# Perceiver block: attention as one run over 128 batches, the work of three groups placed between its matmuls, and the 257th context row added once per group

## What is computed

```python
x = x + xattn(layernorm(x), ctx)      # 8 heads of 64; keys and values are the 257 context rows
x = x + decay(layernorm(x))           # per row: w,k,v,r projections and a scan over the 32 rows
x = x + ffn(layernorm(x))             # 256 -> 64 -> 1024 (gelu) -> 64 -> 256, bias b2

# xattn
attn = softmax((x @ Wq) @ (ctx @ Wk).T * 64**-0.5); out = (attn @ (ctx @ Wv)) @ Wo + bo
# decay, with its own layernorm inside (ln_g, ln_b)
state = (1 - w)[..., None] * state + k[..., None] * v[..., None, :]; out_t = r . state
```

## Time and profile before

| | |
|---|---|
| median of 3 runs | 1327.41 us (1326.62 to 1332.69) |
| the profiled execution's own time | 1328.87 us |
| its span, first to last instruction | 1327.1 us |
| mean granted TensorE clock | 0.972 |
| PE busy, 7368 matmuls | 1194.7 us, 90% of the span |
| DVE, ACT, POOL busy | 636.4 us (48%), 621.4 us (47%), 245.3 us (18%) |
| DMA | 73.85 MB, mean 56 GB/s |
| busiest lines on PE | L476 140.1, L440 132.2, L443 90.2, L480 85.9, L463 82.8 us |
| tail lines on PE | L454 58.8, L478 58.1, L481 51.4 us |

### The profile page before, as it was taken

How to read it: one execution, slowest core, us unless ns; L and a number is a source line. 1 busy time by engine, 2 the same in 40 slices (tenths; PEclk the granted TensorE clock), 3 DMA queues, 4 the chain that set the end, 5 groups by cost and what they waited for, 6 DMA issues and landing times.

```text
span 1327.1 us, 23547 instructions
## 1 busy us (share of the span) xinstructions
PE 1194.7 (90%) x7368; PEld 845.4 (64%) x7368; DVE 636.4 (48%) x2083; ACT 621.4 (47%) x1502; POOL 245.3 (18%) x276
## 2 busy tenths in 40 slices
PE   3889999998999999999999999999999999989865
PEld 2556666676666667666666766666666666766644
DVE  2326455363644536355462645536363553636442
ACT  2444463645546454453645446364543636455321
POOL 0012021121211212121121212112120211212030
PEclk9999999999999999999999999999999999999976
DMA  6212113030210302112030211203021130302000
GB/s 211 71 51 64 58 45 85 8 102 17 71 56 25 98 13 82 37 58 70 22 100 14 76 43 47 81 15 101 12 72 56 44 84 8 94 26 65 28 8 8
DMA packets 49684, 73.85 MB, mean 56 GB/s; under 512 B 5696, under 2 KB 31424, under 8 KB 49664
## 3 DMA queue, kind: packets, MB, share of 16 engines
q1 hardware_dynamic: 42464, 65.06, 17.0%
q10 hardware_dynamic: 7200, 8.53, 1.9%
HBM read 68.98 MB, written 4.59 MB: 55 GB/s over the span
## 4 chain that ended last, share of the span: by engine, by line
PE 40%; issue 36%; POOL 8%; ACT 8%; DVE 6%; ACTq 1%; DMA 0%; POOLq 0%; SPq 0%; DVEq 0%
PE gb L513 7%; PE gb L503 4%; PE scores L440 4%; PE gb L416 4%; PE scores L443 3%; POOL khat L1051 3%; PE gb L425 3%; PE gb L578 2%; PE acc L476 2%; PE ptp L463 2%; PE acc L480 2%; POOL rstd L1024 2%; POOL rhat L1043 2%; PE gb L569 1%; PE scores L454 1%
## 5 line engine op out<-in xcount | busy, mean ns | idle before, releaser
L662 ACT ACTIVATE probs<-scores,nmax 128x257 f32<-128x257 f32 x256 | 119.4, 472 | 209.8 <-DVE nmax L847 209.6
L847 DVE TENSOR_REDUCE nmax<-scores 128x1 f32<-128x257 f32 x256 | 96.9, 420 | 241.9 <-PE scores L454 135.9
L678 ACT ACTIVATE pc<-acc 128x512 f32<-128x512 f32 x128 | 76.5, 598 | 175.1 <-PE acc L481 175.1
L1024 POOL TENSOR_TENSOR rstd<-ve,vecs 128x2 f32<-128x2 f32 x48 | 35.3, 736 | 607.8 <-DVE ve L831 607.8
L476 PE MATMUL acc<-pt,raw_n 128*128 128x256 f32 x512 | 140.1, 396 | 0.6 <-ACT pt L674 0.6
L440 PE MATMUL scores<-raw_t,qk 128*128 128x257 f32 x512 | 132.2, 381 | 1.4 <-ACT qk L698 1.4
L945 DVE COPY_PREDICATED s<-mask,gb 128x256 f32<-128x256 uint8 x256 | 112.6, 442 | 13.7 <-issue 8.3
L463 PE MATMUL ptp<-ident_r,probs 128*128 128x128 f32 x512 | 82.8, 287 | 24.5 <-DVE probs L854 24.5
L476 PEld LDWEIGHTS acc<-pt,raw_n 128*128 128x128 f32 x512 | 90.9, 190 | 20.2 <-issue 3.2
L440 PEld LDWEIGHTS scores<-raw_t,qk 128*128 128x128 f32 x512 | 88.5, 190 | 9.3 <-issue 1.7
L674 ACT ACTIVATE pt<-ptp 128x512 f32<-128x512 f32 x128 | 76.0, 594 | 37.3 <-PE ptp L463 35.9
(11 more groups left out here) (117 smaller groups left out, 2405.0 us busy)
## 6 DMA issues: line engine op xcount, KB each, us to landing
raw_t<-in_ctx_t SPq DMA_DIRECT2D x128, 258.0 KB, 2.8
raw_n<-in_ctx_n SPq DMA_DIRECT2D x128, 192.0 KB, 2.3
xin<-in_x SPq DMA_DIRECT2D x16, 256.0 KB, 2.9
out<-vt ACTq DMA_DIRECT2D x16, 256.0 KB, 3.4
tailc<-tail_scratch SPq DMA_DIRECT2D x64, 6.0 KB
wq<-in_wq SPq DMA_DIRECT2D x1, 512.0 KB, 3.6
wk_raw<-in_wk SPq DMA_DIRECT2D x1, 512.0 KB, 4.1
wo<-in_wo ACTq DMA_DIRECT2D x1, 512.0 KB, 5.4
```

The source lines that it names most:

```text
L662: go(probs[:, r, 0:L], scores[:, r, 0:L], ACT.Exp, bias=nmax[:, r:r + 1], accum_out=rsum[:, r:r + 1]).then_inc(s["exp_ready"], 1)
L678: go(pc[:, :, :, b * S:(b + 1) * S], acc[:].rearrange("p c (h s) -> p c h s", h=H), ACT.Copy).then_inc(s["pc_ready"], 1)
L847: v_.tensor_reduce(nmax[:, r:r + 1], scores[:, r, 0:L], AX.X, ALU.max, negate=True)\
```

## The change

- The phases and the loop go. PE, ACT, DVE and POOL run through one unrolled sequence of slots (i, b), i from -1 to 17; while batch n = 8i+b has its attention, the slot's fills come from group i+1 (queries), i-1 (`WV Y1 XT2 z k r v Sa`) and i-2 (`Sb O2 Y2`, ffn).
- The block `START` goes: all its steps stand in `FILL1` and `FILL2`. Eight batches of attention follow the eight before them directly. The steps of DVE and POOL have tables of their own.
- The 257th row: `turn_tail`, `ptt`, L478, L481, `tail_parts` and the `tailc` loads go. In their place the values of all 257th rows (`VT`) are computed once; POOL sorts each batch's last column into `ptm` (`tail_column`, 32 elements a row); once per group PE turns it (`TP`, two products of 32 columns), DVE spreads it (`psp`) and `WV` gets four more products (K = 64, 256 columns) with `vsp`, which 16 small DMAs on SP fill per group.
- `nmaxs` becomes one reduction of 2x257, `norm_probs` one TENSOR_TENSOR with a broadcast `rinv` in place of two scalings. `probs`, `qk`, `x12` are double, `raw_t` and `raw_n` threefold, and all other tiles have memory of their own.
- The second power chain on POOL goes (the norm of a normed row is folded into epsilon). The softmax scale moves from `wk` to ACT's drain of `q`.
- ACT issues 24 loads at the start (`wq`, 8 small, 15 weights); SP issues the stores; `xb` has its own load.

```diff
-START = ["WV0", "WV1", "XT", "XT3", "Pf", "q0", "q1", "H0", "H1", "Y1", "Qk0", "Qk1", "q2", "H2", "H3", "Qk2", "Qk3",
-         "q3", "Qk4", "Qk5", "XT2", "Qk6", "Qk7", "z"]
-FILL1 = [["k"], ["r"], ["v"], ["Sa0", "Sa1"], ["Sa2", "Sa3"], ["Sb0", "Sb1"], ["Sb2", "Sb3"], ["O2"]]
-FILL2 = [["Y3"], [], [], [], [], [], [], ["Y2"]]
+FILL1 = [["WV"], ["Y1"], ["q0", "q1", "XT2"], ["z", "k"], ["r", "q3"], ["Qk2", "Qk4", "Pf"], ["v", "H0"],
+         ["TP", "Qf", "Sa0"]]
+FILL2 = [["Sb0"], ["Sb2", "XT"], ["q2", "O2"], ["Y2"], ["Qk0", "XT3"], ["Qk6"], ["H2"], ["Sa2", "Y3"]]
...
-                    if b > 0:
-                        turn_tail(b - 1, "scores_ready")
...
-                    mm(acc[:, 0], tailc[:, b % 4, 0:P], ptt[:], start=False, stop=True)
...
-                    last = mm(acc[:, 1], tailc[:, b % 4, P:2 * P], ptt[:], start=False, stop=True)
...
+            def turn_tails(g):
+                out_ = tile("TP", g)
+                pe.wait_ge(s["ptm_ready"], (g + 1) * G)
+                for r in range(2):
+                    last = mm(out_[:, 0, 0:S], ptm[g % 2][:, r].rearrange("p a b h -> p (a b h)"), diag[:],
+                              start=r == 0, stop=r == 1)
+                done("TP", g, last)
...
+                    last = [mm(out_[p][:, i], vsp[64 * p:64 * p + 64, (4 * p + 2 * i) * DH:(4 * p + 2 * i + 2) * DH],
+                               psp[64 * p:64 * p + 64].rearrange("p b s -> p (b s)"), start=False, stop=True)
+                            for p in range(2)]
...
+            for i in range(FIRST, LAST + 1):
+                for b in range(G):
+                    n = i * G + b
+                    before, behind = fills(i, b)
+                    if 0 <= n < B:
+                        turn_probs(n)
+                    if 0 <= n + 1 < B:
+                        score(n + 1)
+                    for name, g in before:
+                        steps[name](g)
+                    if 0 <= n < B:
+                        pv(n)
+                    for name, g in behind:
+                        steps[name](g)
...
+                for h in range(H):
+                    cols = slice(h * DH, (h + 1) * DH)
+                    for half in range(2):
+                        sp.dma_start(vsp[half * 64 + h:half * 64 + 64:H, cols], scratch[g * G:(g + 1) * G, cols])\
+                            .then_inc(vsp_in, 16)
...
+            for i in range(0, LAST + 2):
+                for b in range(G):
+                    n = i * G + b
+                    if b == 1 and 0 <= i - 3 < NG:
+                        store(i - 3)
+                    if b == 2 and i < NG:
+                        load_xb(i)
+                    if b == 5 and i < NG:
+                        load_tail_values(i)
+                    if b == 7 and i + 2 < NG:
+                        load_x(i + 2)
+                    if n + RING < B:
+                        load_t(n + RING)
+                        load_n(n + RING)
...
+            def nmaxs(n):
+                dve.wait_ge(s["scores_ready"], 2 * n + 2)
+                v_.tensor_reduce(nmax[:], scores[:, :, 0:L], AX.X, ALU.max, negate=True)\
+                    .then_inc(s["nmax_ready"], 1)
...
+                v_.tensor_tensor(p_[:, :, 0:L], p_[:, :, 0:L],
+                                 rinv[:].rearrange("p (r o) -> p r o", o=1).to_broadcast([P, 2, L]),
+                                 ALU.mult).then_inc(s["probs_ready"], 1)
...
+            GAPS = [[["Sa2-2", "Sa3-2"], [], ["Y3-3"]],
+                    [["Sb0-2", "Sb1-2"], [], ["Y1-1"]],
+                    [["xn1-1", "Sb2-2", "Sb3-2"], [], []],
+                    [[], [], ["f1-1", "f2-1", "f3-1", "i1-1", "i2-1"]],
+                    [["Y2-2"], ["xn2-2"], ["i3-1", "pw-1", "bw-1", "k1-1", "b1-1"]],
+                    [["p1-1"], [], ["b2-1"]],
+                    [["p2-1"], [], ["ln0+2"]],
+                    [["xn0+2"], ["psp+0"], ["Sa0-1", "Sa1-1"]]]
...
+                p_.tensor_tensor(ptm[g % 2][:, :, :, b],
+                                 probs[n % 2][:, :, L - 1:L].rearrange("p r (o u) -> p r o u", o=1)
+                                 .to_broadcast([P, 2, 2, H]), head[:], ALU.mult).then_inc(s["ptm_ready"], 1)
...
+            STEPS = [[[], []], [[], ["ln1-1"]], [[], []], [[], []], [["ln2-2"], ["k0-1", "xb+0"]],
+                     [["r1-1", "k2-1"], ["r0-1"]], [["r2-1", "k3-1"], ["ln0+2"]], [["r3-1"], ["ob-2"]]]
```

More of the change, by code:

```diff
@@ L74 @@
[L74 to L115, removed]
@@ L142 @@
-class Chain:
[L145 to L151, removed]
+RING = 3
+BANKS = 4
+PREP, HERE, POST, FFN = 1, 0, -1, -2
+FILL1 = [["WV"], ["Y1"], ["q0", "q1", "XT2"], ["z", "k"], ["r", "q3"], ["Qk2", "Qk4", "Pf"], ["v", "H0"],
+         ["TP", "Qf", "Sa0"]]
@@ new lines @@
+FILL2 = [["Sb0"], ["Sb2", "XT"], ["q2", "O2"], ["Y2"], ["Qk0", "XT3"], ["Qk6"], ["H2"], ["Sa2", "Y3"]]
+TILES = {"WV": ["WV0", "WV1"]}
+for pair in ("Qk0 Qk1", "Qk2 Qk3", "Qk4 Qk5", "Qk6 Qk7", "H0 H1", "H2 H3", "Sa0 Sa1", "Sa2 Sa3", "Sb0 Sb1",
+             "Sb2 Sb3"):
+    TILES[pair.split()[0]] = pair.split()
+SHIFT = {"XT": PREP, "TP": HERE}
+SHIFT.update({f"q{p}": PREP for p in range(4)})
+SHIFT.update({f"Qk{h}": PREP for h in range(H)})
+SHIFT.update({n: POST for n in "WV Y1 XT2 z k r v Sa0 Sa2".split()})
@@ L213, in build @@
[L213 to L219, removed]
+        qk = [sb(f"qk{i}", [P, 2, G, 256]) for i in range(2)]
+        pc = sb("pc", [P, 2, H, T])
+        ptm = [sb(f"ptm{i}", [P, 2, 2, G, H]) for i in range(2)]
@@ new lines, in build @@
+        psp = sb("psp", [P, G, S])
+        vsp = sb("vsp", [P, INNER])
+        xin, xn0, xt1 = sb("xin", [P, 2, D]), sb("xn0", [P, 2, D]), sb("xt1", [P, 2, T])
+        qs = sb("qs", [P, 4, T])
+        stats, mv = sb("stats", [P, 3, 2, 6]), sb("mv", [P, 3, 2, 2])
+        ve, rstd, half = sb("ve", [P, 3, 2]), sb("rstd", [P, 3, 2]), sb("half", [P, 2])
+        o_ = sb("o", [P, 4, T])
+        xb = sb("xb", [P, 2, D])
+        x12 = [sb(f"x12_{i}", [P, 2, D]) for i in range(2)]
+        xn1, xt2 = sb("xn1", [P, 2, D]), sb("xt2", [P, 2, T])
@@ new lines, in qf_, with y3 @@
+            def qf_(g):
+                out_ = tile("Qf", g)
+                drained("H3", g)
+                for c in range(8):
+                    r0 = 64 * (c % 2)
+                    last = mm(out_[r0:r0 + 64, 0], u2[:, c], hid[:, c], start=c < 2, stop=c > 5)
+                done("Qf", g, last)
+            def y3(g):
+                out_ = tile("Y3", g)
+                drained("Qf", g)
+                for t in range(2):
+                    last = mm(out_[:, t], qf[:, t * P:(t + 1) * P], v2[:], start=True, stop=True)
+                done("Y3", g, last)
@@ new lines, in wait_tile, with drain, exps @@
+            def wait_tile(name, g):
+                bank, k = BANK[name, g]
+                act.wait_ge(bank_filled[bank], k)
+                return gb[bank]
+            def drain(name, g, last):
+                last.then_inc(bank_drained[BANK[name, g][0]], 1)
+            def exps(n):
+                act.wait_ge(s["nmax_ready"], n + 1)
+                if n > 1:
+                    act.wait_ge(s["ptm_ready"], n - 1)
+                for r in range(2):
+                    go(probs[n % 2][:, r, 0:L], scores[:, r, 0:L], ACT.Exp, bias=nmax[:, r:r + 1],
+                       accum_out=rsum[:, r:r + 1]).then_inc(s["exp_ready"], 1)
```

1296 lines of the change are left out of this document (574 added, 722 removed).

## The result

| | before | changed |
|---|---|---|
| median of the runs, us | 1327.01 | 1265.2 (1261.3 to 1271.74) |
| ratio (95%) | | 0.9531 (0.9481 to 0.958) |
| profiled execution, its span, us | 1328.87, 1327.1 | 1261.3, 1259.2 |
| mean granted clock of the span | 0.972 | 0.957 |

A forecast was written before the change was run, and what follows sets the result against it. PE's passes, then exposed chains once per turn, were taken as the bound. 30.4 + 49.3 + 59.7 + 892 (13 full groups of 68.6) + 60.2 + 73 = 1164.6 us span, so 1165 us; range 1140 to 1192.

The forecast's parts named there:

- slot 5: In b=5 of a full group the maxima start some 1 us late and PE stands about 1.2 us at Pf.
- slot 7: In b=6 and 7 Qf waits 0.55 us for ACT's last gelu; in b=7 late x loses 0.2 us.
- the rival from SP: Sixteen vsp transfers on SP make PE wait from 0.94 us each; at 1.7 each, 1333 us; chance 0.03.
- the port rival: POOL hinders each batch's new scaling, 1.0 us later in 13 or so slots without cover: 1178 us; chance 0.04.
- the clock: Full groups: no wait as long as the 1.69 us behind which the granted clock fell, so no clock loss.
- the waits stay: In-order engines and a four-tile ring leave 6 us of waits in a group instead of 2: 1221 us; chance 0.18.
- the clock falls again: If PE's stand at b=5 nears 1.7 us, 1.7 us more per group: 1189 us; chance 0.05.
- The joints: PE's matmuls of a full group, switches priced as today: 66.6 us, 65 to 68 with more alternation.
- i = 1: Second group of attention, without ffn and Sb O2 Y2: 56.7 + 3 = 59.7 us.
- i = 15: Last group of attention, no queries to make, 8.4 us less: 60.2 us.
- i = 0: First group of attention, few fills, five slots as long as the softmax chain, late x costs 3: 49.3 us.
- The run-out: Behind the last attention, from WV on: 73 us (70 to 79), where today takes 76.4.

The follow-up runs named there:

- x2: Changed kernel with x of the group after next asked for at b = 0 instead of b = 7: 1232.43 us, 0.9264.
- x4: Changed kernel with three edits together (p1 behind the maxima of b = 5, x asked for at b = 0, Pf behind the product with the context): 1164.89 us, 0.8767.
- c0: Changed kernel run again without an edit: 1261.49 us, 0.9486.
- e7: Changed kernel with the 257th row left out of the product with the context (no TP, psp, vsp, ptm): 1253.72 us, 0.9468.
- x5: Changed kernel with POOL's xb moved from slot 4 to slot 7: 1226.65 us, 0.9232.
- e6: Kernel before the change with the 257th row left out of the product with the context: 1237.39 us, 0.9311.
- x1: Changed kernel with DVE's p1 behind the maxima of b = 5 instead of ahead of them: 1211.77 us, 0.9114.
- x3: Changed kernel with Pf behind the product with the context of slot 5 instead of ahead of it: 1213.54 us, 0.9119.

## Why the prediction was right and wrong

**Right.** The direction and the places. The exposed chain at the turn's ends did go: PE has no wait on the row's path in the full groups, and no full group waits for `probs`. What is late next was named correctly for slot 5, `Pf` behind `Qk2` and the cause DVE's list ahead of the maxima. In slot 7 the place is right and the cause half: I gave 0.55 us to the gelus and 0.2 to the late x, and `x2` shows that all 0.8 us come from x. `WV` took 5.02 (5.1), `TP` 0.56 (0.45), the first scores came at 27.1 (26.2). SP's sixteen small transfers take 0.54 us each in the median, 8.7 a group, and nobody waits for a context: the rival from SP, which needed 0.94, is off.

```profile
L242 SPq DMA_DIRECT2D vsp<-tail_values x256: 542/543/1081, 60.2 to 1159.9; - x128
L688 DVE TENSOR_TENSOR probs<-probs,rinv x128: 694/695/696, 30.9 to 1166.6; 128x514 f32<-128x514 f32 x128
```

The second row is the scaling, 694 to 696 ns all 128 times, never hindered: the port rival doesn't hold where I put it.

**The step that failed: slot 5.** "The maxima start some 1 us late", and so "PE stands about 1.2 us". They start some 2.7 late, and PE stands 3.2: 1.7 us later than I had it, and 2.0 longer. I had the price for a hindered product, 1.69 instead of 0.69, and let one product pay it. The timeline of before has the same four products, two of them hindered, at 1.69 + 1.40 + 0.42 + 0.43 = 3.94 us:

```profile
429.06 1.69 DVE L905 TENSOR_TENSOR at<-bwd,fw 128x512 f32<-128x512 f32 x1
432.27 1.40 DVE L910 TENSOR_TENSOR khat<-kt,at 128x512 f32<-128x512 f32 x1
434.71 0.42 DVE L917 TENSOR_TENSOR at<-at,pw 128x256 f32<-128x256 f32 x1
435.16 0.43 DVE L925 TENSOR_TENSOR pw<-pw 128x256 f32<-128x256 f32 x1
```

In the new order POOL is at work beside all four, and they take 6.05 us. The port rival was real, only at the decay's products instead of the scaling.

**The step that fell with it: the clock.** "Neither is as long as the 1.69 behind which the clock fell, so no clock loss." The wait was 3.2, not 1.2, and the clock falls at it in 11 of the 13 full groups, five times for 3.4 us and six times for 6.8. Against the group without a fall (72.2 us) such groups take 73.5 to 73.8 and about 75.0 where their waits are the same, so a fall costs some 1.5 or 2.8 us: 24 us in all, 1.9 a group. Two rivals came true together, "the waits stay" in part (4.2 us, not 6) and "the clock falls again"; I had treated them as alternatives, though by the second one's own condition a long wait brings both. A group: 67.97 of matmuls + 3.2 at `Pf` + 0.8 for `qf` + 0.2 for the copies of `s` + 1.9 of clock = 74.1, with 74.2 measured.

**The joints**, a term of the sum that was mis-sized: 67.97 instead of 66.6. The attention of a batch is 3.63 instead of 3.48, as the removal of L478 left 0.96 for L356 (four passes beside the switch), 0.11 less than with it and not 0.22; 8 x 0.15 = 1.2 of the 1.4. The trace of before had a sign of it: in its turn at full clock (416.3 to 493.5) PE is busy for 72.4 us, where the same prices made 70.3.

**i = 1**: 66.4 for 59.7; the late x cost 6 us (`x2`: 60.4), where I had 3, and 2.8 more go with the other two edits (57.6). **i = 15**: 66 for 60.2; it takes 64.5 to 66.9 in every run with the row. I had subtracted the 8.4 us of passes that it doesn't make, but without them some slots are no longer covered, and PE waits for the softmax as in i = 0:

```profile
1160.38 1.11 PE L345 MATMUL ptp<-ident,probs 128*128 128x128 f32 x4 [4.78 <-DVE probs L688]
```

**The run-out**: 80.5 for 73. The waits of over 0.7 us in it add up to 19.4 us, against 24.6 before, so the order is better, as I had taken it without a row; but the clock is 0.77, and PE is busy for 55.4 us, where it had 48.6. With the three edits the waits are the same 19.4 and the clock is 0.85: 75.3 us. So 5 of the 7.5 us go with the clock. Why the clock differs there stays open; a change of order there is not needed for it, as `x2`, whose edit touches nothing there, takes 76.4.

The forecast of 1165 us and `x4`'s 1164.9 agree by chance: 8.3 us too many in the full groups (26 for waits that are gone, less 18 for the joints) and 3.7 in i = 0 and 1 stand against 1.9 too few at the start, 5.8 in i = 15 and 2.3 in the run-out. What holds of it is that a group's matmuls allow 68 us.

## What to carry to other kernels

Where engines run an order written by hand, look at what stands ahead of the one instruction that a chain waits for, and move all that isn't needed behind it; ask for a load as soon as its place is free; and put an instruction that needs no tile of a scarce ring between those that do. When you cost a list of DVE products beside work of POOL, take the hindered time for every one of them, not for one. A long wait can cost itself and a half-speed stretch behind it (here some 1.5 or 2.8 us), so the edit that shortens it can gain more than the wait.

## What the runs showed of the hardware

- The granted clock falls to 0.50 for 3.4 or 6.8 us at some waits and not at others of the same length. In how many of the 13 full groups or turns it falls at the wait named:

| run | the wait, once in each | falls |
|---|---|---|
| changed, `c0`, `x2` | 3.2 us, `Pf` | 11, 10, 11 |
| `e7` | 3.2 us, `Pf` | 6 |
| `x5` | 2.2 us, `Pf` | 4 |
| before | 1.7 us, the tail | 11 |
| `e6` | 1.7 us, `probs` | 2 |
| `x1`, `x3` | 1.6 us, `Pf` | 0, 0 |

Within one kernel a shorter wait goes with fewer falls; across kernels it does not (before against `e6`, the changed kernel against `e7`). In `x1` one fall follows a wait of 1.4 us for `qf`. What decides beside the length, no run shows.

- Four DVE products with two inputs, in a row beside POOL's, took 6.05 us; the earlier trace rows has 0.69 for one of them alone, and `b1` alone takes 0.42. By its place `xn`, which has one large input, was hindered too: at 585.35 its two halves take 1.60 us together while POOL runs a product from 585.21 for 1.27, and 0.41 each in the kernel before.
- The matmul time of a group with every wait gone repeats to 0.01 us over twelve groups (67.97), while in the changed kernel they spread from 72.2 to 76.4.
